# Rows of small feed-forward tiles turned by VectorE's block transpose of four extra loads, in place of TensorE with the identity

## The reference

```
x = layernorm(x + attention(x))          # 16 heads of 8; probabilities mixed with a copy that has key 0 left out
x = layernorm(x + mixture_of_experts(x)) # 8 experts, two per token
# expert e:  h = silu(x @ w1[e].T) * (x @ w3[e].T);  out += weight[e] * (h @ w2[e].T)     # F = 512
```

## Time and profile before

| what | value |
|---|---|
| time, median of 3 runs | 1200.72 us (1200.65 to 1201.82) |
| profiled execution: span from first to last instruction | 1199.0 us |
| TensorE busy | 1121.4 us, 94% |
| VectorE busy | 917.7 us, 77% |
| ScalarE busy | 828.0 us, 69% |
| GpSimd busy | 660.1 us, 55% |
| first and last L1293 (VectorE turns a whole tile) | 777.2 and 1075.6 us |
| first and last L698 (TensorE turns a small tile) | 1081.2 and 1143.8 us |
| last scatter issued (L1646) | 1152.36 us |

### The profile page before, as it was taken

How to read it: one execution, slowest core, us unless ns; L and a number is a source line. 1 busy time by engine, 2 the same in 40 slices (tenths; PEclk the granted TensorE clock), 3 DMA queues, 4 the chain that set the end, 5 groups by cost and what they waited for, 6 DMA issues and landing times.

```text
span 1199.0 us, 23515 instructions
## 1 busy us (share of the span) xinstructions
PE 1121.4 (94%) x7114; PEld 563.5 (47%) x7117; DVE 917.7 (77%) x1328; ACT 828.0 (69%) x1689; POOL 660.1 (55%) x999
## 2 busy tenths in 40 slices
PE   4899999999999999999999999899999999999986
PEld 3322222222322222322322222278999999999952
DVE  6778999999999999999999999854445544443334
ACT  2278889888888888888889888844443344345636
POOL 4314446676676676676676654666545433433335
PEclk9989999999999999999999999999999999999998
DMA  5433443443543444444444454353334433321146
GB/s 161 136 100 111 118 116 112 134 132 107 145 126 109 144 119 118 132 130 122 130 124 125 123 144 154 96 112 82 87 76 100 90 78 75 77 63 42 41 164 265
DMA packets 170077, 138.46 MB, mean 115 GB/s; under 512 B 84563, under 2 KB 146647, under 8 KB 169952
## 3 DMA queue, kind: packets, MB, share of 16 engines
q1 hardware_dynamic: 160064, 117.22, 36.7%
q0 software_dynamic: 8688, 18.14, 4.6%
q10 hardware_dynamic: 1200, 1.57, 0.5%
HBM read 94.59 MB, written 42.19 MB: 114 GB/s over the span
## 4 chain that ended last, share of the span: by engine, by line
PE 46%; DVE 39%; issue 9%; DMA 2%; SPq 2%; POOL 1%; ACTq 1%; ACT 0%; POOLq 0%; DVEq 0%
DVE rowmax_sb L998 31%; PE ring_ps L741 10%; PE mx_ps L722 10%; PE mx_ps L712 9%; PE ring_ps L607 5%; PE acc_ps L619 4%; PE mx_ps L596 3%; DVE TN_sb L1007 3%; PE mx_ps L773 2%; PE ring_ps L652 1%; DVE stats_sb L1030 1%; DVE meanvar_sb L1037 1%; PE ring_ps L660 1%; DMA bo_sb<-bo 1%; SPq L522 1%
## 5 line engine op out<-in xcount | busy, mean ns | idle before, releaser
L795 ACT ACTIVATE probs_sb<-ring_ps 128x512 f32<-128x512 f32 x1024 | 558.1, 598 | 99.2 <-PE ring_ps L607 83.9
L998 DVE TENSOR_REDUCE rowmax_sb<-mx_ps 128x4 f32<-128x2048 f32 x256 | 585.9, 2289 | 33.1 <-PE mx_ps L596 28.0
L607 PE MATMUL ring_ps<-region_sb 74*128 74x512 bf16 x1024 | 313.7, 388 | 2.5 <-ACT probs_sb L795 2.2
L619 PE MATMUL acc_ps<-probs_sb,values_sb 128*32 128x512 f32 x2048 | 273.2, 606 | 0.0
L1646 POOL DMA_INDIRECT y_d<-probs_sb,values_sb x135 | 133.0, 985 | 197.4 <-DVE probs_sb L1311 172.9
L607 PEld LDWEIGHTS ring_ps<-region_sb 74*128 74x128 bf16 x1024 | 79.3, 97 | 318.2 <-ACT probs_sb L795 274.1
L879 ACT ACTIVATE xT_sb<-region_sb 128x512 f32 x78 | 49.2, 630 | 186.2 <-PE mx_ps L722 184.8
L1524 POOL DMA_INDIRECT rows_d<-sent_sb,pos_sb x128 | 130.1, 1016 | 41.1 <-issue 19.2
L1319 DVE TENSOR_TENSOR probs_sb<-mx_ps,probs_sb 128x1024 f32<-128x1024 f32 (+1 forms) x78 | 84.3, 1081 | 77.9 <-PE mx_ps L722 77.9
L596 PE MATMUL mx_ps<-k_maxima_sb,q_maxima_sb 32*128 32x512 bf16 x1024 | 102.2, 389 | 41.9 <-DVE rowmax_sb L998 41.5
L741 PE MATMUL ring_ps<-region_sb,probs_sb 128*128 x1080 | 135.9, 278 | 3.9 <-DMA region_sb<-w2T 2.3
(11 more groups left out here) (183 smaller groups left out, 1163.5 us busy)
## 6 DMA issues: line engine op xcount, KB each, us to landing
region_sb<-k_parts_d SPq DMA_DIRECT2D x64, 288.0 KB
region_sb<-q_parts_d SPq DMA_DIRECT2D x60, 288.0 KB
k_parts_d<-k_parts_sb SPq DMA_DIRECT2D x48, 256.0 KB, 2.5
k_maxima_sb<-k_parts_d SPq DMA_DIRECT2D x256, 32.0 KB
probs_sb<-y_d SPq DMA_DIRECT2D x32, 256.0 KB, 5.3
q_maxima_sb<-q_parts_d SPq DMA_DIRECT2D x244, 32.0 KB
values_sb<-rows_d SPq DMA_DIRECT2D x57, 132.0 KB, 2.3
q_parts_d<-q_parts_sb SPq DMA_DIRECT2D x16, 384.0 KB, 3.6
```

The lines of the kernel that those rows point to most:

```text
L607: nc.tensor.matmul(bank, KS[b % 2][0:KR + MR, h, P * c:P * (c + 1)], QS[b % 2][0:KR + MR, h, :], start=True, stop=True).then_inc(s_ring_re ...
L619: last = nc.tensor.matmul(acc_ps[VW * j:VW * (j + 1), 0, :], VE[b % 2][:, c, HG * g + j, :], PT[u % 2][:, j, c, :], start=(c == 0), stop=( ...
L795: nc.scalar.activation(PT[u % 2][:, i // QC, i % QC, :], ring_bank("st", u, i), ACT.Exp, scale=SCALE).then_inc(s_ring_done, 1)
L998: V.tensor_reduce(rowmax[u % 2][:, :].rearrange("p (j c) -> p j c", c=QC)[:, :, c], mx_ps[:, :, :], axis=AXX, op=ALU.max, negate=True).the ...
```

## The change

Small tiles take the way of whole tiles. SP loads their blocks too, with half as many rows, and then the rows of two tiles before, up to the last tile; VectorE turns them; TensorE's transposes, their PSUM half bank and ScalarE's copies go, with their two semaphores. `tile_up` waits for `s_turned` for every tile.

```diff
@@ load_blocks (SP)
-                    sp.dma_start(XB[t % BRING][VW * i:VW * (i + 1), :].rearrange("s (j r) -> s j r", r=VW),
-                                 rows_d[bass.ds(row, TK), VW * i:VW * (i + 1)].rearrange("(j s) r -> s j r", s=VW))\
+                    sp.dma_start(blocks(t)[VW * i:VW * (i + 1), :].rearrange("s (j r) -> s j r", r=VW),
+                                 rows_d[bass.ds(row, P * halves(t)), VW * i:VW * (i + 1)].rearrange("(j s) r -> s j r", s=VW))\
...
+        def blocks(t):
+            return XB[t % BRING][:, 0:P * halves(t)]
@@ SP's loop
-            for t in range(TILES):
+            for t in range(TILES + 2):
...
-                if t < FULL:
+                if t < TILES:
                     load_blocks(t)
-                for n in range(t - 2 if t <= FULL else t, t - 1 if t < FULL else t + 1):
-                    if is_tile(n):
-                        load_rows(n)
+                if t >= 2:
+                    load_rows(t - 2)
@@ TensorE
-            def small_tile_in(t):
-                pe.wait_ge(*rows_in(t))
-                for w in range(halves(t)):
-                    last = nc.tensor.transpose(xgt_ps[:, TK * (t % 2) + P * w:TK * (t % 2) + P * (w + 1)],
-                                               XG[t % RING][:, w, 0:P], ident[:, :])
-                last.then_inc(s_xgt_ready, 1)
 
             def tile_up(t):
-                if t < FULL:
-                    pe.wait_ge(s_turned, t + 1)
-                else:
-                    pe.wait_ge(s_xgt, t - FULL + 1)
+                pe.wait_ge(s_turned, t + 1)
...
                 beside(t, 0)
-                if FULL <= t + 1 < TILES:
-                    small_tile_in(t + 1)
                 if is_tile(t - 1):
                     tile_down(t - 1)
@@ ScalarE
-            def small_tile_in(t):
-                act.wait_ge(s_xgt_ready, t - FULL + 1)
-                n = P * halves(t)
-                nc.scalar.activation(XGT[t % 2][:, 0:n], xgt_ps[:, TK * (t % 2):TK * (t % 2) + n], ACT.Copy)\
-                  .then_inc(s_xgt, 1)
...
-                if FULL <= t + 1 < TILES:
-                    small_tile_in(t + 1)
@@ VectorE
-                V.transpose(XGT[t % 2][:, :], XB[t % BRING]).then_inc(s_turned, 1)
+                V.transpose(XGT[t % 2][:, 0:P * halves(t)], blocks(t)).then_inc(s_turned, 1)
...
-                if t + 1 < FULL:
+                if t + 1 < TILES:
                     turn_rows(t + 1)
```

More of the change, by code:

```diff
@@ L203, in layer @@
         up_ps, lin_ps = (mx_ps[:, 2 * n:2 * n + 2, :].rearrange("p k (c q) -> p (k c) q", q=TK) for n in range(2))
-        xgt_ps, y_ps = ring_ps[0][:, 0, :], ring_ps[1][:, 0, :]
+        y_ps = ring_ps[1][:, 0, :]
         def tile_by_expert(first, last):
@@ L250, in layer @@
         s_xb_in = [sem(f"row_blocks_loaded{n}") for n in range(BRING)]
-        s_turned, s_xgt_ready, s_xgt = sem("rows_turned"), sem("xgt_ready"), sem("xgt_drained")
+        s_turned = sem("rows_turned")
         s_up, s_lin, s_silu, s_h = sem("up_ready"), sem("lin_ready"), sem("silu_done"), sem("h_done")
```

## The result

The change made the kernel slower: 1208.25 us (1203.57 to 1210.47, 4 runs) against 1201.1 (1200.65 to 1201.82), a ratio of 1.0051, 95% interval 1.0034 to 1.0068, so 4 to 8 us. Timed again beside other kernels it took 1207.94 us, ratio 1.0054 (1.0040 to 1.0067). Predicted were 1205.5 us, +4.8, in a range of 1200.5 to 1209.5.

The account below looks back on a forecast made before the run. Small tiles were taken as bound by the loop of down, lin and product, then by SP's queue once its lead was spent: 1.4 + 4.5 - 0.95 - 0.1 = +4.8, so 1205.5 us, range 1200.5 to 1209.5.

Parts of the forecast that it names:

- The loop of 2.99 us: Small tiles: down, lin, product and the next down wait on each other in a round of 2.99 us.
- the transposes worth nothing: TensorE, small tiles: transposes stand in the loop's gap; removing 21 gains nothing in steady rounds, 0.10 us in all.
- VectorE's turning at 0.30: VectorE, small tiles: each added block transpose takes 0.30 us behind a product, cost 0 while its data are there.
- SP's time per tile, 3.68: SP's queue, small tiles: 3.68 us a tile running free, 0.69 more than the loop lasts.
- A block load of half the size at 0.30: SP's queue, small tiles: 0.30 us for a half-size block load against 0.317, so 0.95 us less.
- The lead: SP runs ahead through four block buffers: 8.3 us from tile 63, shrinking 0.69 a tile, used up at tile 75.
- the undisturbed loss: Small tiles to tile 77: SP's excess beyond its lead, without stretched loads, 14 x 0.69 - 8.3 = 1.4 us.
- Held loads, 4.5 us: SP's queue from tile 63 on: block load groups stretched by 0.30 us each over 15 tiles, 4.5 us.
- a landing of 2.0 throughout: Small tiles' row loads: data taken to land at the median 2.0 us after issue.
- (a): Rival: SP keeps up, small block loads well under 0.30 or stretches fall away; only -0.1 remains, 1200.6 us; chance 0.20.
- (b): Rival: TensorE was the bound, the transposes' slots leave the period; 6.3 us faster, 1194.4 us; chance 0.05.
- (c): Rival: small block loads on SP are dear, 0.59 us each; +21 us, 1222; chance 0.07.

Follow-up runs that it names:

- e1: Kernel before with the small tiles' transposes and ScalarE copies taken out and nothing put in: 1202.58 us, ratio 1.0009.
- e6: Kernel before with lin(t) ahead of down(t-1) in small tiles from 58 on, lin's results in two PSUM banks: 1197.28 us, ratio 0.9971.
- e2: Kernel after with only two of the four block loads for each small tile: 1202.93 us, ratio 1.0007.
- e3: Kernel after with one value load a tile on SP in place of two, all DMAs kept: 1200.32 us, ratio 0.9984.
- e9: Kernel after with three block buffers in place of four, the last w2 quarter's load kept at position 4: 1211.66 us, ratio 1.0081.
- e4: Kernel after run again unchanged, beside other kernels on one chip: 1207.94 us (1207.36 to 1211.82, 5 runs).

## Why the prediction was right

It was right in direction, in where the time goes and, roughly, in size; the size owes something to errors that offset each other. The sizes of single terms follow.

- The loop of 2.99 us and the transposes worth nothing: shown by e1 (59.69 us either way) and by e6, where a change of order, with a second bank for lin, shortens the round.
- VectorE's turning at 0.30, without cost: 0.301 at the least, and e2 and e3 carry all of it at the time of before.
- SP's time per tile, 3.68: 3.72. The row load takes 0.357 (median) for the 0.338 of the earlier trace rows.
- A block load of half the size at 0.30, 0.95 us less: mis-sized. Loads of either size take 0.317 at the median, so the term is 0. The rule of the Trainium skill that would have made it 0.16 (in "Perfetto Trace Analysis", "DMA Instruction — HWDGE (DVE, Sync)": the profiled time holds the descriptors' generation) does not show here as a time in proportion to the descriptors: half as many, the same time.
- The lead: blocks(63) were to begin 1.63 us after the product of tile 57; they began 1.65 after it (1089.69 and 1088.04). With 3.72 a tile the undisturbed loss is 14 x 0.735 - 8.3 = 2.0 us for the 1.4 of the sum. e3, with a shorter time per tile, and e9, with a shorter lead, confirm it from both sides.
- Held loads, 4.5 us: the groups from tile 63 on are over 1.81 by 1.5 us in all in the first trace of the kernel after and by 3.7 in the second, and two short pauses of 0.3 came with each. In the first, 2.0 + 1.5 + 0.6 = 4.1, measured 3.96. In the second, 2.0 + 3.7 + 0.6 = 6.3 of 8.41; of the rest 1.4 is one row load, that of tile 75, that took 3.3 us to land where 1.9 is the median. The prediction had a landing of 2.0 throughout: its spread was a term left out. So was TensorE's clock: behind an idle of 2.53 us before a late down the granted clock falls to 0.50, the weight loads of the last lin take 1.82 us for 0.97, and the last round is 3.92 for 2.98, 0.9 more. With it the terms come to 8.6. Both rows are of e4:

```profile
1156.67 1.82 PEld L715 LDWEIGHTS mx_ps<-k_parts_sb,full_k_sb 128*128 128x128 f32 x8
```

```profile
1157.00:1159.00 2.00, 1.78 (x9) 1.49 (x7) 0.46 (x2) 0.00 (x0) 0.70 (x1) 0.50 0.01 0
```

The medians are 6.1 and 7.2 us up for the 4.8 of the sum. The undisturbed loss was taken too small by 1.5 us (1.4 - 0.95 for 2.0), the held loads and pauses too large by 0.2 to 2.4 (4.5 for 4.3 and 2.1), and late landing and the clock were left out; that the sum comes so near the medians is in part luck. No trace of a run near the median was taken, so the shares there are not shown. Rivals (a), (b) and (c) are excluded by the waits for DMA in the trace, by e1, and by the 0.317.

## What to carry to other kernels

Before an instruction is taken off the busiest engine, look whether it stands in a gap: follow one round through the engines by start times, and if another chain adds up to the same period, the saving is nothing until that chain is cut (here lin ahead of down, 3 us of 1200). A load moved onto a queue has to be priced at that queue's free-running pace, value loads, register work and holds included, against the period of the stage it feeds; buffers only lend a lead, which a longer stage spends. When a position in a loop hangs on a buffer count, changing the count changes more than the buffers.

## What the runs showed of the hardware

SP's price for a block load did not depend on its size here: 0.316 us at the least and 0.317 at the median for loads of 32 KB and of 16 KB. That of a row load did a little: 0.395 for 256 rows, 0.357 for 128. On the queue a block load is worth more than its record: e2, with two fewer, has a tile time of 2.73 for 3.72, so 0.50 each. A value load with its register work is worth 0.66 us of the queue (3.72 a tile, 3.06 in e3), more than one such load, and leaving one out a tile is the whole difference between 1207.9 and 1200.3 us.

TensorE's granted clock is not the same in each execution of a program: behind the wait for w2 it fell to 0.50 in the trace of e4, and not in the other one of the same kernel. How long the weight loads had been idle doesn't tell which: it fell after 2.41 us in e3 and not after 2.73 in the kernel before.

Held loads: in the second trace of the kernel after, four of the five longest groups (2.35 to 2.94 us for 1.81; the fifth, at 1136.62, had a packet of the other instruction queue) have a packet that starts in their time on the queue that the profile calls q8 instruction, and an undisturbed group at 1132.90 has none. This is the DMA view of the stretch 1108.5 to 1111.6, around the longest:

```profile
q1 hardware_dynamic: 424, 0.10, 16.8%
q0 software_dynamic: 32, 0.07, 6.2%
q8 instruction: 1, 0.02, 2.3%
```

In the first trace the longest of the small tiles' groups, 3.23 us at 1075.45, has such a packet in its time, and one began 0.6 us before the next, 2.77 at 1093.45; but one also began 0.4 us before a group that was hardly held, 1.90 at 1135.98. So instruction fetches are a candidate for what holds SP's issue, but not shown as the cause; no run took them away.
